# A fused cross attention stage: scores moved behind the next queries, softmax into the same step, turned probabilities ahead of output rows

## The reference

```python
xn = layernorm(x)
q = xn @ Ly[h] + Lo[h]           # 128 -> 64 per head
k = ctx @ Lx[h]
s = (q @ k.T + mask) ; p = softmax(s * scale)
o = p @ (ctx @ Tx[h]) + To0[h]
x = x + sum_h(o @ Ty[h]) + To1
```

## Time and profile before

| | us |
|---|---|
| median of 3 runs | 2528.41 (2522.78 to 2529.38) |
| the profiled execution, its time | 2521.92 |
| the profiled execution, its span | 2520.1 |
| PE busy in the span | 2371.4 (94%) |
| DVE busy in the span | 1904.4 (76%) |
| cross stage: start of step −16 to start of step 0 | 14.60 to 236.93 |
| local stage and the rest | 236.93 to 2520.1 |

### The profile page before, as it was taken

One profiled execution on the slowest core, in us unless ns is written; L12 is line 12 of the kernel. 1 busy time (PEld: TensorE's weight loads), 2 busy tenths in 40 slices (PEclk: granted clock), 3 DMA queues, 4 the chain that ended last, 5 costly groups with the idle time before them and its releaser, 6 DMA issues.

```text
span 2520.1 us, 60784 instructions
## 1 busy us (share of the span) xinstructions
PE 2371.4 (94%) x25500; PEld 1437.9 (57%) x25500; DVE 1904.4 (76%) x3471; ACT 1453.2 (58%) x2047; POOL 1186.5 (47%) x883
## 2 busy tenths in 40 slices
PE   6787899999999999999999999988889999999999
PEld 5666556566665666666665666554555555455443
DVE  4666999999999899999999999965866766455222
ACT  2233566666666666666666666653467677566443
POOL 1222777777677767777767776741211111001000
PEclk9899999999999999999999999999899999999999
DMA  3000000000010000000000000001000101120110
GB/s 123 6 6 8 2 2 2 27 10 13 2 35 2 13 18 18 7 7 27 10 8 7 27 10 11 2 1 75 18 32 15 35 12 40 41 83 20 38 52 28
DMA packets 36164, 56.27 MB, mean 22 GB/s; under 512 B 6380, under 2 KB 20852, under 8 KB 35640
## 3 DMA queue, kind: packets, MB, share of 16 engines
q1 hardware_dynamic: 35896, 52.40, 6.7%
HBM read 51.19 MB, written 1.19 MB: 21 GB/s over the span
## 4 chain that ended last, share of the span: by engine, by line
PE 54%; DVE 28%; ACT 11%; issue 5%; POOL 1%; SPq 0%; DMA 0%; DVEq 0%; ACTq 0%
PE w L1380 9%; PE w L1370 9%; DVE turned L976 4%; DVE norm L983 4%; PE w L643 4%; PE w L624 4%; PE w L634 4%; PE py L658 4%; PE w L413 3%; DVE top L429 3%; DVE straight_odd L971 2%; DVE logit L432 2%; PE w L711 2%; ACT sq L877 2%; PE w L1499 2%
## 5 line engine op out<-in xcount | busy, mean ns | idle before, releaser
L424 ACT ACTIVATE prob<-logit 128x512 f32<-128x512 f32 x224 | 137.5, 630 | 299.0 <-DVE logit L432 299.0
L1370 PE MATMUL w<-qT,m_fc 128*128 128x512 f32 x544 | 267.7, 605 | 0.4 <-ACT turned L1617 0.4
L1122 POOL TENSOR_TENSOR straight_odd<-straight_odd,turned 128x1024 f32<-128x1024 f32 x96 | 227.5, 2370 | 82.5 <-DVE turned L976 79.6
L454 POOL TENSOR_TENSOR prob<-prob,rden 128x1024 f32<-128x1024 f32 x112 | 213.4, 1906 | 99.0 <-DVE rden L443 99.0
L976 DVE TENSOR_TENSOR turned<-w,rot 128x512 f32<-128x512 f32 x384 | 245.3, 680 | 0.0
L1122 POOL TENSOR_TENSOR straight<-straight,turned 128x1024 f32<-128x1024 f32 x96 | 226.6, 2370 | 37.3 <-DVE turned L976 37.3
L1116 POOL TENSOR_TENSOR straight_odd<-straight_odd,rnorms 128x1024 f32<-128x1024 f32 x96 | 180.6, 1903 | 115.3 <-DVE rnorms L997 115.3
L983 DVE TENSOR_REDUCE norm<-sq 128x16 f32<-128x1024 f32 x192 | 224.0, 1207 | 0.0
L1116 POOL TENSOR_TENSOR straight<-straight,rnorms 128x1024 f32<-128x1024 f32 x96 | 180.6, 1901 | 69.9 <-DVE rnorms L997 69.9
L643 PE MATMUL w<-b_wqkv,m_proj 128*128 128x512 f32 x384 | 191.3, 621 | 4.0 <-DVE logit L432 4.0
L890 ACT COPY qT<-w 128x1024 f32<-128x1024 f32 x96 | 97.3, 1014 | 162.0 <-PE w L670 162.0
(11 more groups left out here) (253 smaller groups left out, 5255.5 us busy)
## 6 DMA issues: line engine op xcount, KB each, us to landing
b_wqkv<-gates SPq DMA_DIRECT2D x64, 256.0 KB, 3.7
b_wqkv<-in_b_wqkv SPq DMA_DIRECT2D x18, 512.0 KB, 3.6
ctxT<-in_ctxT SPq DMA_DIRECT2D x64, 64.0 KB, 1.8
b_wo<-in_b_wo SPq DMA_DIRECT2D x6, 512.0 KB, 3.6
m_fc<-in_m_fc SPq DMA_DIRECT2D x1, 2304.0 KB, 9.4
m_proj<-in_m_proj SPq DMA_DIRECT2D x1, 2304.0 KB, 13.0
m_fc<-in_m_fc SPq DMA_DIRECT2D x8, 256.0 KB, 3.5
m_proj<-in_m_proj SPq DMA_DIRECT2D x8, 256.0 KB, 3.4
```

The costliest lines, as they stand in the source:

```text
L454: pool.tensor_tensor(flat, flat, k.rden[:, s, :, None].broadcast_to([P, HEADS, SEQ]), ALU.mult).then_inc(k.prob_ready, 1)
L1122: pool.tensor_tensor(k.straights[s][:, i, :, :], k.straights[s][:, i, :, :], k.turned[:, i, :, :], ALU.add).then_inc(added, 1)
L1370: pe.matmul(claim(("hidden", J, c)), k.m_fc[:, x, c * P:(c + 1) * P], k.m_xT[:, q, :], start=True, stop=True).then_inc(k.ring_full, 1)
```

## The change

In cross steps PE's order becomes: queries of g, (turn_in), scores of g−1, values of g−1, keys of g, turned probabilities of g−2, output rows of g−3, turn of the next x, attention of g−2. The masking, maximum, shift, exponential, sum and division of tile g−1 now run in step g, where those of tile g−2 ran. Keys of tile g now wait for the mask of tile g−1 (`masked`, T), since that is what reads the scores out of `w1`. The rounding of weights is cut in two: `quantise_step` runs early in step −11, the rest in step −10, and the decoding of 8-bit floats moves from step −10 to step −8. The waits of `turn_x` are for the early part alone; the wait for the rounded weights stands before their first use.

```diff
--- before.py
+++ after.py
@@ -317,6 +317,7 @@
         k.quant.turned = sem("quant_turned")
         k.quant.diag = sem("quant_diag")
         k.quant.spread = sem("quant_spread")
+        k.quant.step = sem("quant_step")
         k.quant.done = sem("quant_done")
 
         k.f = Names()
@@ -547,7 +548,7 @@
         if g - 1 == QUANTISE:
             pe.wait_ge(k.quant.diag, 1)
         if g - 2 == QUANTISE:
-            pe.wait_ge(k.quant.done, 1)
+            pe.wait_ge(k.quant.step, 1)
         pe.transpose(k.pt[:, 0:P], k.normed[:, g % 2, :], k.ident[:, :]).then_inc(k.xT_psum, 1)
 
     def cross_queries(g):
@@ -562,8 +563,7 @@
     def cross_keys(g):
         T, s = FIRST + g, g % 2
         pe.wait_ge(k.ctx_loaded[s], 16 * ((g + TILES) // 2 + 1))
-        pe.wait_ge(k.kT_ready, T)
-        pe.wait_ge(k.masked, T - 1)
+        pe.wait_ge(k.masked, T)
         for h in range(PAIRS):
             mm = pe.matmul(k.w1[:, h * P:(h + 1) * P], k.a_lx[:, h * P:(h + 1) * P], k.ctxT[:, s, :],
                            start=True, stop=True)
@@ -580,13 +580,8 @@
         mm.then_inc(k.v_psum, 1)
 
     def cross_scores(g):
-        T = FIRST + g
-        pe.wait_ge(k.qT_ready, T + 1)
-        if is_cross(g + 1):
-            pe.wait_ge(k.kT_ready, T + 2)
-        else:
-            pe.wait_ge(k.kT_ready, T + 1)
-            pe.wait_ge(k.k_turned, T + 2)
+        pe.wait_ge(k.qT_ready, FIRST + g + 1)
+        pe.wait_ge(k.kT_ready, FIRST + g + 1)
         scores_tensor(pe, k, g % 2)
 
     def cross_rows(g):
@@ -638,6 +633,7 @@
     def keys(g):
         T, d = FIRST + g, g // TILES
         pe.wait_ge(k.bk_loaded, 16 * (d + 1))
+        pe.wait_ge(k.masked, FIRST)
         pe.wait_ge(k.shifted, T - 1)
         for c in range(2):
             mm = pe.matmul(k.w1[:, 512 * c:512 * c + 512], shifted_rows(k, g % TILES),
@@ -784,6 +780,7 @@
         if quad_at(g, TURN) is not None:
             quad_in(quad_at(g, TURN))
         if is_cross(g - 1):
+            cross_scores(g - 1)
             cross_values(g - 1)
         elif before:
             values(g - 1)
@@ -791,6 +788,8 @@
             cross_keys(g)
         elif this:
             keys(g)
+        if is_cross(g - 2):
+            turn_probs(g - 2, before)
         if is_cross(g - 3):
             cross_rows(g - 3)
         if p is not None:
@@ -805,12 +804,10 @@
             turn_queries(g - 1, this)
         if hid is not None:
             hidden(hid, 1, g)
-        if before2:
+        if before2 and not is_cross(g - 2):
             turn_probs(g - 2, before)
         if before and g >= 1:
             turn_keys(g - 1, this)
-        if is_cross(g - 1):
-            cross_scores(g - 1)
         if hid is not None:
             hidden(hid, 2, g)
         if before2:
@@ -860,8 +857,8 @@
         T, s = FIRST + g, g % 2
         this, before, before2 = stages_of(g)
         hid = quad_at(g, HIDDEN)
-        if before2:
-            exp_scalar(act, k, T - 2, s, 0.125 if is_cross(g - 2) else 8.0)
+        if before2 and not is_cross(g - 2):
+            exp_scalar(act, k, T - 2, s, 8.0)
         if this and not is_cross(g):
             act.wait_ge(k.q_psum, T + 1)
             act.wait_ge(k.q_norm2, T)
@@ -878,6 +875,8 @@
         if before:
             act.wait_ge(k.v_psum, T)
             act.copy(k.v2[:, 1 - s, :, :], k.w2[:, :]).then_inc(k.v_ready, 1)
+        if is_cross(g - 1):
+            exp_scalar(act, k, T - 1, 1 - s, 0.125)
         if is_cross(g):
             act.wait_ge(k.k_psum, T + 1)
             act.copy(k.kT[:, s, :, :], k.w1[:, :]).then_inc(k.kT_ready, 1)
@@ -929,15 +928,17 @@
         dve.tensor_tensor(k.qT[:, g % 2, :, :], k.w0[:, :].rearrange("p (h n) -> p h n", n=P),
                           k.a_lo[:, :, None].broadcast_to([P, PAIRS, P]), ALU.add).then_inc(k.qT_ready, 1)
 
-    def cross_shift(g):
+    def cross_mask(g):
         T, s = FIRST + g, g % 2
         dve.wait_ge(k.s_psum, T + 1)
         logits = by_pair(k.logit[:, s, :, :])
         dve.tensor_tensor(logits.rearrange("p h a m -> p a h m"),
                           k.w1[:, :].rearrange("p (a h m) -> p a h m", a=2, m=SEQ),
                           k.a_mask[:, None, None, :].broadcast_to([P, 2, PAIRS, SEQ]), ALU.add).then_inc(k.masked, 1)
-        dve.wait_ge(k.masked, T + 1)
-        softmax_shift_vector(dve, k, T, s, logits)
+
+    def cross_shift(g):
+        dve.wait_ge(k.masked, FIRST + g + 1)
+        softmax_shift_vector(dve, k, FIRST + g, g % 2, by_pair(k.logit[:, g % 2, :, :]))
 
     def cross_update(g):
         T, x = FIRST + g, k.x[:, g + TILES, :]
@@ -1047,21 +1048,28 @@
         this, before, before2 = stages_of(g)
         p, hid, out = pair_at(g), quad_at(g, HIDDEN), quad_at(g, OUTPUT)
         local = this and not is_cross(g)
-        if is_cross(g - 2):
-            cross_shift(g - 2)
-        elif before2:
+        if is_cross(g - 1):
+            cross_mask(g - 1)
+            cross_shift(g - 1)
+        if before2 and not is_cross(g - 2):
             dve.wait_ge(k.s_psum, T - 1)
             softmax_shift_vector(dve, k, T - 2, s, k.w1[:, :].rearrange("p (a h m) -> p h a m", a=2, m=SEQ))
         if is_cross(g + 2):
             cross_stats(g + 2)
+        if g == QUANTISE:
+            quantise_spread(dve, k)
+        if g == QUANTISE + 1:
+            quantise_step(dve, k)
         if is_cross(g):
             query_bias(g)
+        if is_cross(g - 1):
+            softmax_sum_vector(dve, k, T - 1, 1 - s)
+        elif before2 and not is_cross(g - 2):
+            softmax_sum_vector(dve, k, T - 2, s)
         if is_cross(g + 2):
             cross_normalise(g + 2)
         if is_cross(g - 4):
             cross_fresh(g - 4)
-        if before2:
-            softmax_sum_vector(dve, k, T - 2, s)
         if local:
             if g % TILES == 0:
                 rotations(g // TILES)
@@ -1094,11 +1102,9 @@
             dve.wait_ge(k.loaded_later, 16 * N_LATER)
             dve.tensor_copy(k.band16[:, :], k.band[:, :])
             quantise_largest(dve, k)
-        if g == QUANTISE:
-            quantise_spread(dve, k)
-        if g == QUANTISE + 1:
+        if g == QUANTISE + 2:
             quantise_weights(dve, k)
-        if g == QUANTISE + 2:
+        if g == QUANTISE + 4:
             fp8_weight_vector(dve, k)
         if is_cross(g - 2):
             output_bias(g - 2)
@@ -1148,7 +1154,9 @@
             add_to1(g)
         if is_cross(g + 2):
             rstd_gpsimd(pool, k, k.norm, T + 2, s)
-        if before2:
+        if is_cross(g - 1):
+            softmax_scale_gpsimd(pool, k, T - 1, 1 - s)
+        elif before2 and not is_cross(g - 2):
             softmax_scale_gpsimd(pool, k, T - 2, s)
         if this and not is_cross(g):
             add(g, 0, k.q_turned, k.q_added)
@@ -1192,10 +1200,15 @@
     dve.tensor_scalar(k.wdiag[:, :], k.ident[0:4, 0:4], k.wmaxT[:, 0:1], None, ALU.mult).then_inc(q.diag, 1)
 
 
+def quantise_step(dve, k):
+    q = k.quant
+    dve.wait_ge(q.spread, 1)
+    dve.tensor_scalar(k.wstep[:, :], k.pt[:, P:P + 4], 1.0 / 127.0, None, ALU.mult).then_inc(q.step, 1)
+    dve.wait_ge(q.step, 1)
+
+
 def quantise_weights(dve, k):
     q, w = k.quant, k.s_w[:, 2, :, :]
-    dve.wait_ge(q.spread, 1)
-    link(dve, k, dve.tensor_scalar(k.wstep[:, :], k.pt[:, P:P + 4], 1.0 / 127.0, None, ALU.mult))
     link(dve, k, dve.reciprocal(k.wrstep[:, :], k.wstep[:, :]))
     wide = (lambda c: c[:, :, None].broadcast_to([P, 4, P]))
     link(dve, k, dve.tensor_tensor(w, w, wide(k.wrstep), ALU.mult))
@@ -1485,6 +1498,8 @@
         mm.then_inc(d.v_psum, 1)
 
     def queries(n, W):
+        if n == 2:
+            pe.wait_ge(k.quant.done, 1)
         pe.matmul(k.pt[:, 2 * P:3 * P], k.s_w[:, n, 0, :], k.xT[:, W % 2, :], start=True, stop=True).then_inc(d.q_psum, 1)
 
     def rows(n, W, u):
```

## The result

The changed kernel took 2496.71 us (median of 4 runs, 2495.75 to 2497.43) against 2526.02 of the kernel before (4 runs). The ratio is 0.9884, 95% interval 0.9866 to 0.9901: 29 us faster, or 25 to 34 by the interval. In it the first query product began at 16.33 us, 1.7 later than before (14.60), because its operands landed later; from the first query to the end the difference is 26.7.

The account below looks back on a forecast made before the run. No engine was taken as full; a ring of waits across tiles bound the cross stage. Cross steps and the stretch before gain 30.4 us, the passage loses 4.0: 26.4 us, from 2528.41 to 2502.0; range 2491 to 2516.

Parts of the forecast that it names:

- The ring goes, PE sets the step: Cross steps: softmax and attention of successive tiles no longer wait on each other in a circle; PE's work sets the length.
- 12.4 us a step: Cross steps: PE's start-to-start distances plus 1.60 us from turn of x to attention sum to 12.4 us.
- Rounding 4.0: Steps −10 and −8: rounding and decoding of weights on DVE delay oT beyond its slack, costing 4.0 us, bounds 0 and 6.
- the half microseconds of steps −13 and −12: Steps −13 and −12: reductions and copies for the rounding take around half a us each beyond DVE's slack.
- The hold-up beside GpSimd: Cross steps on DVE: fresh rows, reading two SBUF tiles, wait for GpSimd's scaling until 12.35, leaving oT 1.07 us of slack.
- Before step −13: 2.0: Step −14 begins 0.7 us later but lasts 11.0 against 13.71 us, gaining 2.0 us.
- The passage, 4 us with bounds 0 and 6: Steps 0 and 1, from cross into local stage: DVE's new waits less softmax work leaving step 1 lose 4 us.
- Clock rival: Cross steps: 1.3 us idle before attention lowers PE's clock, costing 22 us, so no change at 2524; chance 0.10 with other nothing.
- The ring sum of 13.8: Old cross steps: the chain of waits from one tile's oT through softmax to attention and hand-over sums to 13.8 us.
- Half: Cross steps: DVE, not PE, sets the step, adding 1 us each, 13 us: 2515; chance 0.09 including partly cold.
- more: Whole kernel: no rounding stall and nothing handed back in the passage, 34.4 us gained: 2494; chance 0.04.
- slower: The 96 local steps: a worse rhythm between PE and DVE, at 0.5 us each 18 us slower, 2546; chance 0.04.

Follow-up runs that it names:

- e5_filler: Kernel before, with 16 unused identity transposes added in PE's idle time behind the turn of x in each cross step; 2522.47 us, ratio 0.9984.
- e1_split_only: Kernel before, with only the rounding of weights cut in two and moved, waits included; 2525.57 us, ratio 1.0002.
- e7_exp_ahead: Changed kernel, with ACT's copy of the values and exponentials ahead of the square of keys in step 0 alone; 2496.39 us, ratio 0.9882.
- e8_oT_early: Changed kernel, with DVE's oT of tile −2 ahead of the norms in step 0 alone; 2490.80 us, ratio 0.9862.
- e11_late_passage: Changed kernel, with the turned probabilities back behind the turn of x in steps 0 and 1 alone; 2491.13 us, ratio 0.9861.
- e10_all_late_passage: Changed kernel with ACT's probT before xT, normalisations before sums, step 0's exponentials and oT early, turned probabilities late in steps 0 and 1; 2477.74 us, ratio 0.9805.
- e12_late_rest: Changed kernel with turned probabilities late in all steps, normalisations before sums, step 0's exponentials and oT early, ACT's probT order kept; 2486.95 us, ratio 0.9848.

## Why the prediction was right

Forecast were 26.4 us and 2502.0; measured 29.3 and 2496.7, in the range. By its own steps:

- **The ring goes, PE sets the step.** Right: no wait for scaled probabilities is left, and PE's only regular wait is the 1.27 us for `probT`, forecast as 1.3.
- **12.4 us a step.** 12.12 measured. The terms were start-to-start distances of the old order, and these depend on the neighbour: from the turned probabilities to the next group it is 0.87 us now (0.99 taken), from the scores 1.09 (1.18), from the turn of x to attention 1.54 (1.60). That is 0.27 a step, 3.5 in 13. For the first two the difference is not PE's wait before them, but, as far as the rows show, what follows them: 64 x 64 products in the old order, products over all 128 rows in the new one. In `e5_filler` the transposes of step −8 follow the filler at once (134.45) and the scores still begin 1.00 us later.
- **Rounding 4.0.** The waits for oT in steps −9 and −7 were 1.69 and 1.08, 2.8 in sum; the half microseconds of steps −13 and −12 did not come. The rounding itself took 2.65 us of DVE (92.47 to 95.12) in place of 3.5. The hold-up beside GpSimd was as said, 2.03 us for the fresh rows. The clause that the split takes stalls away was right, but as `e1_split_only` shows, the split alone gains nothing that the total can tell.
- **Before step −13: 2.0.** 2.1 measured, with some luck: `e7_exp_ahead`, `e8_oT_early` and `e11_late_passage` have the same code up to there and gained 1.0 to 1.8.
- **The passage, 4 us with bounds 0 and 6.** 8.0 measured: this is the step that failed. Its first terms held: DVE idle for the scores 2.21 (2.3 said) and for the exponentials 2.43 (2.6 said), and the rotation tables did not wait for GpSimd. The key squares cost 3.84 in place of 2.2, since I let PE work at full clock behind six us of idle time, and at the end DVE waited 4.65 for ACT's logarithm where I had 1.1 for attention. The four waits of DVE, less the 5.3 us of softmax work that left step 1, sum to 7.8, close to the measured 8.0. The prediction let the values of step 1 wait for the late oT "as before". That was a misreading: before, they followed the queries at once, and the wait of 6.03 us is new. `e8_oT_early`, which takes 4.5 us of it away, shows it as the cause of most (5.9 us of the total).
- **Clock rival.** Refused: 1.3 us of idle time in 12 leaves the granted clock at 1.00. But the forecast did not say how much of the gain the clock is; `e5_filler` shows 7.0 of 20.3 us over nine steps. The ring sum of 13.8 was right for step −13; from step −12 on the ring is 14.06, since the sum left out the fresh rows. So what lengthened the old steps was not two things but three.
- **Half, more, slower.** DVE did not take over (in step −6 oT begins at 144.32, values want it at 146.57). The 88 local steps from 4 to 92 took the same time within 0.4 us, so the slower rhythm did not come.

The errors of the cross stage (5.2 us too little gained) and of the passage (4 us too little lost) partly cancelled. That the total was closer than its parts is luck: step 2 began 25.8 us earlier than before, where 26 was said, although step 0 began at 203.10, where near 206.5 was said.

## What to carry to other kernels

Where no engine is full, add up the ring of waits across tiles: its sum gave the step length (13.8 us, and 14.06 with the fresh rows, to the measured 13.80 and 14.06), and breaking it at one place, by running a stage in the step of its own scores, gave 2 us a step. A stall that is worth next to nothing inside a ring is worth its full length, and the clock behind it, once the ring is gone; so test the parts of a change in the order in which they stand. A moved instruction only helps if its consumer's queue lets it (the early turned probabilities gave nothing behind ACT's copy of x): look at the in-order queue of the next engine, and at the steps at which two stages meet.

## What the runs showed of the hardware

- Idle time of 2.3 to 3.4 us in steps of 13.3 to 15.5 let the granted clock fall in some steps of the kernel before and not in others; filled with 2 us of transposes the clock stayed at 1.00 through nine steps. With 1.3 us idle in 12.12 it stayed at 1.00, after 6.03 it fell, and the next products took 3.68 and 3.12 us for 1.94 and 1.98. The length of the wait alone does not decide: behind the same idle time of 3.74 us the turned queries of step 1 took 1.97 us in `e10_all_late_passage` and 1.09 in `e12_late_rest`.
- A VectorE subtraction and product of 128 x 128 with two SBUF inputs took 2.03 us beside GpSimd's scaling, and 0.35 in the kernel before, where it ran clear of it. It ended 0.14 us after GpSimd's instruction. In step 0 of the changed kernel, where the fresh rows (214.40) began ahead of GpSimd's scaling (214.56), they took 0.26 us and the scaling 2.19 in place of 1.90.
- The first products of an execution began at 14.3 to 16.6 us from the start of the span among the fourteen profiles, by when their operands landed. Traces of two kernels are best compared from the first product, not from zero.
